# Causal attention with 16 heads: the mask added by VectorE on the way out of PSUM

## The reference, cut to what matters

```python
x = x + xattn(layernorm(x), ctx, ctx, ...)      # x, ctx: (16, 128, 256)
x = x + ffn(layernorm(x), w_fc, b_fc, w_proj, b_proj)

def xattn(q, k, v):                              # 16 heads of 16 features
    qh, kh, vh = q @ Wq.T + bq, k @ Wk.T + bk, v @ Wv.T + bv
    qh, kh, vh = (t.reshape(B, 16, 128, 16) for t in (qh, kh, vh))
    scores = einsum('bhqd,bhkd->bhqk', qh, kh) / sqrt(16)
    scores = where(triu(ones(128, 128), k=1), -inf, scores)
    out = einsum('bhqk,bhkd->bhqd', softmax(scores), vh)
    return out.reshape(B, 128, 256) @ Wp.T + bp

def ffn(x):                                      # 256 -> 1024 -> 256
    h = gelu(quant(x) @ quant(w_fc).T + b_fc)
    return quant(h) @ quant(w_proj).T + b_proj   # 3-bit mantissas, blocks of 32
```

## Time and profile before

| what | value |
|---|---|
| median of 3 runs | 295.81 us |
| the profiled execution | 296.32 us, span 294.3 us |
| PE busy | 248.6 us (84%) |
| PE weight loads | 176.6 us (60%) |
| DVE busy | 206.1 us (70%) |
| ACT busy | 168.0 us (57%) |
| POOL busy | 62.0 us (21%) |
| granted TensorE clock, mean | 0.915 |

### The profile page before, as it was taken

The page is one execution under the profiler, slowest core; times in us unless marked ns, Lnnn a source line. Parts: engine busy times, 40 slices in busy tenths (PEclk is TensorE's granted clock), DMA queues, the critical chain, the costliest instruction groups (busy, mean ns, idle before and its releaser), DMA issues.

```text
span 294.3 us, 6286 instructions
## 1 busy us (share of the span) xinstructions
PE 248.6 (84%) x2121; PEld 176.6 (60%) x2128; DVE 206.1 (70%) x435; ACT 168.0 (57%) x439; POOL 62.0 (21%) x54
## 2 busy tenths in 40 slices
PE   2764998998799899899999899788967974998853
PEld 1553776777577577578677677555733653565532
DVE  5400557979528857856956864896868999999991
ACT  2330665856726846855964864576843553676641
POOL 5200000000000100100100100335032354555551
PEclk9995799999779999999999799989775898699998
DMA  6457746755784565465555545443013001111111
GB/s 202 111 101 150 197 107 101 233 111 109 141 180 82 95 125 109 82 111 123 91 103 124 90 55 121 96 52 57 0 23 51 0 18 38 36 36 36 36 37 53
DMA packets 92436, 26.64 MB, mean 91 GB/s; under 512 B 69492, under 2 KB 92160, under 8 KB 92416
## 3 DMA queue, kind: packets, MB, share of 16 engines
q1 hardware_dynamic: 91328, 25.33, 42.3%
q10 hardware_dynamic: 1088, 1.05, 1.1%
HBM read 13.77 MB, written 8.39 MB: 75 GB/s over the span
## 4 chain that ended last, share of the span: by engine, by line
PE 51%; DVE 13%; ACT 11%; issue 9%; DMA 6%; SPq 5%; POOL 2%; POOLq 1%; ACTq 1%; DVEq 0%
PE bank L969 9%; PE bank L916 9%; ACT prob L411 7%; PE bank L980 7%; PE bank L963 4%; PE bank L1005 4%; PE bank L925 4%; PE bank L1123 3%; SPq L302 3%; PE bank L992 3%; DVE h_amax L841 2%; DMA scratch<-full 2%; PE bank L1121 2%; PE bank L1150 2%; DMA oden<-oT 2%
## 5 line engine op out<-in xcount | busy, mean ns | idle before, releaser
L411 ACT ACTIVATE prob<-bank,negm 128x128 f32<-128x128 f32 x256 | 69.6, 390 | 10.6 <-DVE negm L690 10.6
L690 DVE TENSOR_REDUCE negm<-bank 128x4 f32<-128x512 f32 x64 | 41.2, 685 | 42.6 <-PE bank L969 42.6
L417 ACT COPY probT<-bank 128x512 f32<-128x512 f32 x32 | 18.7, 583 | 52.0 <-PE bank L980 52.0
L969 PEld LDWEIGHTS bank<-k_mem,q_mem 16*128 16x128 f32 x512 | 33.7, 197 | 14.0 <-issue 14.0
L969 PE MATMUL bank<-k_mem,q_mem 16*128 16x128 f32 x512 | 40.1, 294 | 0.0
L980 PE MATMUL bank<-ident_f,prob 128*128 128x128 f32 x256 | 38.3, 297 | 0.0
L582 POOL TENSOR_TENSOR hq<-hrn,h_mag 128x1024 bf16<-128x1024 f32 x16 | 30.7, 1919 | 33.3 <-DVE hrn L852 33.3
L980 PEld LDWEIGHTS bank<-ident_f,prob 128*128 128x128 f32 x256 | 30.2, 150 | 4.0 <-issue 0.2
L963 PE MATMUL bank<-mask,ident_b 128*128 128x512 bf16 x64 | 19.8, 391 | 15.1 <-ACT prob L411 9.1
L505 ACT COPY hqT<-bank 128x1024 bf16<-128x1024 bf16 x16 | 16.2, 1012 | 20.3 <-PE bank L1138 20.3
L992 PE MATMUL bank<-probT,V 128*32 128x128 f32 x512 | 23.8, 290 | 3.9 <-DVE probT L695 3.2
(11 more groups left out here) (107 smaller groups left out, 397.2 us busy)
## 6 DMA issues: line engine op xcount, KB each, us to landing
scratch<-full SPq DMA_DIRECT2D x16, 256.0 KB, 3.1
oden<-oT SPq DMA_DIRECT2D x64, 64.0 KB, 2.5
k_mem<-scratch SPq DMA_DIRECT2D x32, 64.0 KB, 2.8
scratch_v<-vrow SPq DMA_DIRECT2D x16, 128.0 KB
q_mem<-scratch SPq DMA_DIRECT2D x32, 64.0 KB, 2.5
V<-scratch_v SPq DMA_DIRECT2D x16, 128.0 KB, 3.3
out<-res SPq DMA_DIRECT2D x16, 128.0 KB, 1.7
cbuf<-in_ctx SPq DMA_DIRECT2D x6, 256.0 KB, 3.2
```

The lines of the kernel that those rows point to most:

```text
L411: ins = nc.scalar.activation(prob[:, k % 4, g, :], score_b[k % 2][:, g * P:(g + 1) * P], ACT.Exp, bias=negm[:, k % 2, g:g + 1])
L690: V.tensor_reduce(negm[:, k % 2, :], score_b[k % 2][:, :].rearrange("p (g t) -> p g t", g=4), axis=AX.X, op=ALU.max, negate=True).then_inc ...
L969: ins = T.matmul(score_b[n][:, g * P:(g + 1) * P].rearrange("p (r j) -> p j r", r=RPH), QS[par][rows, cols], KS[par][rows, cols], start=Fa ...
```

## The change

The causal mask leaves PE and goes to DVE. The queries are scaled by -1/4 instead of 1/4, so the score banks hold negated scores, and the mask holds +1e30 above the diagonal. For each head DVE runs one fused instruction (`tensor_tensor_reduce`): it reads 128 x 128 negated scores out of PSUM, adds the mask, writes the sum to the head's slot of `prob` in SBUF, and keeps the row minimum, which is the negated row maximum of the scores. The exponentials then read and write `prob` in SBUF, with scale -1. `scores` of the next round waits for `masked` (the DVE instructions), no longer for `exp_done`. The wait for a free slot of `prob` moves from ACT to DVE. Both copies of the transposes are on ACT. `negm` has four slots instead of two.

```diff
@@ -47,7 +47,7 @@
         ident_b = sb("ident_b", [P, P], bf16)
         perm_f = sb("perm_f", [P, P])
         ones_b = sb("ones_b", [65, P], bf16)
-        mask = sb("mask", [P, P], bf16)
+        mask = sb("mask", [P, P])
         col_i = sb("col_i", [P, P], i32)
         col_f = sb("col_f", [P, P])
         colp_i = sb("colp_i", [P, P], i32)
@@ -61,6 +61,7 @@
         rowt_f = sb("rowt_f", [P, 1])
         neg_half = sb("neg_half", [P, 2])
         tick = sb("tick", [P, 1])
+        ticks = sb("ticks", [P, 4])
 
 
         w_rows = sb("w_rows", [P, 3, KC, E])
@@ -104,7 +105,7 @@
         QS = [sb(f"q_mem{n}", [P, NG // NR * P * HL]) for n in range(2)]
         KS = [sb(f"k_mem{n}", [P, NG // NR * P * HL]) for n in range(2)]
         V1 = [sb(f"V1_{n}", [P, 2, NH, 2 * HD]) for n in range(2)]
-        negm = sb("negm", [P, 2, 4])
+        negm = sb("negm", [P, 4, 4])
         prob = sb("prob", [P, 4, 4, P])
         probT = sb("probT", [P, 2, 4, P])
         oT = [sb(f"oT{n}", [P, NJ, 2, 4, RPH]) for n in range(2)]
@@ -144,7 +145,7 @@
             iota perm_set row_cast col_cast row_bits consts bias_scaled wT_in wT_out wp_permuted b_parts b_moved
             ones_set bn1 ag1 eps1 pow1 xn_ready tx_done tx_copied tc_done tc_copied
             proj_done proj_copied v_copied k_spilled q_spilled v_spilled q_stacked k_stacked v_stacked
-            s_done max_done exp_done t_done even_copied odd_copied av_done
+            s_done masked max_done exp_done t_done even_copied odd_copied av_done
             o_copied o_moved lden_done rden_done newton onrm_done y_done y_copied
             bn2 ag2 eps2 pow2 xn2_done amax2 exp2 mag2 round2 xq_done
             w_amax_done w_exp_done w_mag_done w_round fc_ready wtr_done wtr_copied
@@ -368,7 +369,7 @@
                     ins = nc.scalar.activation(grouped,
                                                proj_b[t][:, c * PT:(c + 1) * PT]
                                                .rearrange("p (r g h) -> p r g h", r=RPH, h=HL),
-                                               ACT.Identity, scale=(1.0, SCALE)[t],
+                                               ACT.Identity, scale=(1.0, -SCALE)[t],
                                                bias=bias_q[:, c:c + 1] if t else bias[:, 0, c:c + 1])
                 ins.then_inc(sm["proj_copied"], 1)
 
@@ -404,18 +405,21 @@
             copy_tc(1)
 
             def exps(i, k):
-                act.wait_ge(sm["max_done"], GROUPS * i + k + 1)
-                if k >= 4 or from_step(i, 1):
-                    act.wait_ge(sm["t_done"], GROUPS * i + k - 3)
+                act.wait_ge(sm["masked"], 4 * (GROUPS * i + k + 1))
                 for g in range(4):
-                    ins = nc.scalar.activation(prob[:, k % 4, g, :], score_b[k % 2][:, g * P:(g + 1) * P],
-                                               ACT.Exp, bias=negm[:, k % 2, g:g + 1])
+                    ins = nc.scalar.activation(prob[:, k % 4, g, :], prob[:, k % 4, g, :],
+                                               ACT.Exp, bias=negm[:, k % 4, g:g + 1], scale=-1.0)
                 ins.then_inc(sm["exp_done"], 1)
 
             def copy_even(i, j):
                 act.wait_ge(sm["t_done"], GROUPS * i + 2 * j + 1)
                 nc.scalar.copy(probT[:, 0, :, :].rearrange("p g t -> p (g t)"), probT_b[0][:, :])\
                     .then_inc(sm["even_copied"], 1)
+
+            def copy_odd(i, j):
+                act.wait_ge(sm["t_done"], GROUPS * i + 2 * j + 2)
+                nc.scalar.copy(probT[:, 1, :, :].rearrange("p g t -> p (g t)"), probT_b[1][:, :])\
+                    .then_inc(sm["odd_copied"], 1)
 
             def invert(p):
 
@@ -443,6 +447,7 @@
             def step(i, par):
                 if from_step(i, 1):
                     copy_even(i - 1, 3)
+                    copy_odd(i - 1, 3)
                 exps(i, 0)
                 exps(i, 1)
                 if from_step(i, 1):
@@ -450,6 +455,7 @@
                 if ahead(i):
                     copy_proj(i + 1, 0)
                 copy_even(i, 0)
+                copy_odd(i, 0)
                 exps(i, 2)
                 exps(i, 3)
                 if ahead(i):
@@ -457,6 +463,7 @@
                 if is_last(i):
                     copy_weights(0)
                 copy_even(i, 1)
+                copy_odd(i, 1)
                 exps(i, 4)
                 exps(i, 5)
                 copy_out(i, 0, par)
@@ -464,6 +471,7 @@
                     invert(i - 1)
                     copy_weights(1)
                 copy_even(i, 2)
+                copy_odd(i, 2)
                 exps(i, 6)
                 exps(i, 7)
                 if is_last(i):
@@ -477,6 +485,7 @@
 
             steps(act, step)
             copy_even(NPAIR - 1, 3)
+            copy_odd(NPAIR - 1, 3)
             copy_out(NPAIR - 1, 1, 1)
 
             def gelu(t, par):
@@ -648,10 +657,10 @@
             norm1(0)
             V.tensor_scalar(ident_b[:, :], col_f[:, :], row_f[:, :], None, ALU.is_equal).then_inc(sm["consts"], 1)
             dve.wait_ge(sm["row_cast"], 4)
-            V.tensor_scalar(mask[:, :], col_f[:, :], rowt_f[:, :], -BIG, ALU.is_gt, ALU.mult)\
+            V.tensor_scalar(mask[:, :], col_f[:, :], rowt_f[:, :], BIG, ALU.is_gt, ALU.mult)\
                 .then_inc(sm["consts"], 1)
             dve.wait_ge(sm["bias_in"], 64)
-            V.tensor_scalar(bias_q[:, :], bias[:, 1, :], SCALE, None, ALU.mult).then_inc(sm["bias_scaled"], 1)
+            V.tensor_scalar(bias_q[:, :], bias[:, 1, :], -SCALE, None, ALU.mult).then_inc(sm["bias_scaled"], 1)
             stats1(1)
             norm1(1)
             copy_v(0)
@@ -687,13 +696,13 @@
             def maxes(i, k):
 
                 dve.wait_ge(sm["s_done"], GROUPS * i + k + 1)
-                V.tensor_reduce(negm[:, k % 2, :], score_b[k % 2][:, :].rearrange("p (g t) -> p g t", g=4),
-                                axis=AX.X, op=ALU.max, negate=True).then_inc(sm["max_done"], 1)
-
-            def copy_odd(i, j):
-                dve.wait_ge(sm["t_done"], GROUPS * i + 2 * j + 2)
-                V.tensor_copy(probT[:, 1, :, :].rearrange("p g t -> p (g t)"), probT_b[1][:, :])\
-                    .then_inc(sm["odd_copied"], 1)
+                if k >= 4 or from_step(i, 1):
+                    dve.wait_ge(sm["t_done"], GROUPS * i + k - 3)
+                V.memset(ticks[:, k % 4:k % 4 + 1], 0.0)
+                for g in range(4):
+                    V.tensor_tensor_reduce(prob[:, k % 4, g, :], score_b[k % 2][:, g * P:(g + 1) * P], mask[:, :],
+                                           1.0, 3.0e38, ALU.add, ALU.min, negm[:, k % 4, g:g + 1])\
+                        .then_inc(sm["masked"], 1)
 
             def normalise(p):
 
@@ -778,8 +787,6 @@
                 one = type(i) is int and i == 1
                 maxes(i, 0)
                 maxes(i, 1)
-                if from_step(i, 1):
-                    copy_odd(i - 1, 3)
                 if from_step(i, 2):
                     normalise(i - 2)
                 if zero:
@@ -790,7 +797,6 @@
                     round_weights(0, 2)
                 maxes(i, 2)
                 maxes(i, 3)
-                copy_odd(i, 0)
                 if zero:
                     bias_parts(1)
                     copy_wp()
@@ -804,7 +810,6 @@
                     round_weights(1, 3)
                 maxes(i, 4)
                 maxes(i, 5)
-                copy_odd(i, 1)
                 if ahead(i):
                     copy_v(i + 1)
                 if zero:
@@ -818,7 +823,6 @@
                     round_weights(0, 3)
                 maxes(i, 6)
                 maxes(i, 7)
-                copy_odd(i, 2)
                 if zero:
                     round_weights(0, 0)
                 if one:
@@ -830,7 +834,6 @@
                     residual(i - 1)
 
             steps(dve, step)
-            copy_odd(NPAIR - 1, 3)
             quantise(NPAIR - 2)
 
 
@@ -958,16 +961,13 @@
             def scores(i, j, par):
 
                 if j or from_step(i, 1):
-                    pe.wait_ge(sm["exp_done"], GROUPS * i + 2 * j)
-                for n in range(2):
-                    T.matmul(score_b[n][:, :], ident_b[:, :], mask[:, :].unsqueeze(1).to_broadcast([P, 4, P]),
-                             start=True, stop=False)
+                    pe.wait_ge(sm["masked"], 4 * (GROUPS * i + 2 * j))
                 for g in range(4):
                     for n in range(2):
                         b, hs = heads(2 * j + n)
                         rows, cols = head_rows(b, hs[g])
                         ins = T.matmul(score_b[n][:, g * P:(g + 1) * P].rearrange("p (r j) -> p j r", r=RPH),
-                                       QS[par][rows, cols], KS[par][rows, cols], start=False, stop=(g == 3))
+                                       QS[par][rows, cols], KS[par][rows, cols], start=True, stop=True)
                         if g == 3:
                             ins.then_inc(sm["s_done"], 1)
 
```

## The result

The changed kernel took a median of 292.13 us (291.35 to 292.51, 4 runs) against 295.38 us before (294.16 to 300.44, 4 runs). The ratio is 0.990 with a 95% interval of 0.986 to 0.994, so it is about 1% faster, which lies within the 2% band of no change. In a later session the same pair gave 0.980 (0.975 to 0.985). The forecast was 293.5 us.

What follows compares the result with a forecast made beforehand. A ring of ACT and SP, 22.4 us against PE 19.1 and DVE 20.7, was to set the step. 1.9 + 2.4 - 1.8 = 2.5 us off 296.3 gives 293.8, forecast as a median of 293.5, range 290 to 299.

Steps and rivals of the forecast that it cites:

- ring around PE: ACT and SP, query spill to query spill through moves, logarithm and exponentials: sets the step, 22.4 us against 22.77 before.
- steps 0 and 1: Step 0 is PE work and gains up to 2.4 us without masks; step 1, nearly DVE's, loses 1.8.
- steps 2 to 6: Middle steps: each 0.37 us shorter, 5 x 0.37 = 1.9 us in all.
- The ring's sum: ACT and SP, query spill to query spill: terms add up to 22.4 us, with ends at 21.6 and 23.4.
- spill to landed moves: SP, query spill to landing of the eight attention output moves: 12.3 us taken, from 13.1 or 12.1 with quick moves.
- pair of 0.33: DVE, fused instruction plus 128 x 1 readout: 0.33 us, between 0.24 and 0.42; round 2.7, DVE's step 20.7.
- The rival of a bound DVE: DVE becomes the bound: pair of 0.44, round 3.58, step 24.2 us, kernel slower at 308; chance 0.20.
- The source in SBUF: ACT's exponentials reading SBUF: at most 0.05 us more each, 0.6 taken for the 16 in the ring around PE.
- PE's masks: PE loses mask matmuls of 0.60 us a round, 2.4 a step, so it needs 19.1 us instead of 21.5.
- PE's clock: Rival: more PE idle time brings low-clock stretches that catch the query projection, 10.4 us on top, 304; chance 0.12.
- the mark of 0.9: PE: a granted clock under 0.9 in 84 to 165 us would show that the falling-clock rival holds.
- my last warning: SP's queue: the forecast fails if the value gathers, last in it, come late for the attends, which now run earlier.

## Why the prediction was right, and where it was not

**That a ring around PE holds the changed kernel: right, and one run shows it. That it alone sets the step: not borne out.** The denominators' moves were put first, with every instruction of PE, ACT and DVE in place, and 7.5 us left the changed kernel's median, though in another session; in ratios to the kernel before, 0.950 against 0.980 and 0.990. That number had been forecast from the ring. The logarithm waited for the moves in six steps of the changed kernel, from 0.49 to 3.50 us. Against it stand three forecasts made from the same ring that failed. Taking two copies out of it gave nothing that shows, taking the logarithm off the moves gave nothing in the median, and putting the masks back on PE cost 7 us of the median where the ring allowed 1 to 2.5. PE's work and clock lie so close to the ring that what is taken from either shows only in part. That is what the prediction said of the two, and its sum then went by the longer one alone.

**The size: right, and partly by luck.** The profiled executions differ by 3.8 us of span, and the prediction had 2.5 by four terms. The query copies give them as follows:

| term | forecast | after |
|---|---|---|
| steps 0 and 1 | 2.4 - 1.8 = 0.6 | 0.17 |
| steps 2 to 6 | 1.9 | 1.40 - 0.17 = 1.23 |
| rest of the steps, step 7 above all | 0 | 2.52 - 1.40 = 1.12 |
| feed-forward layer | 0 | 3.8 - 2.52 = 1.3 |

Two terms came out smaller and two were not in the sum at all, and the last of these is no effect of the change.

**The ring's sum: 22.4 forecast, 22.86 in the chain, 22.96 on average.** Its terms on ACT were right. From the landing at 119.98 to the spill at 129.81 it took 9.83 us, where the terms had given 22.4 - 12.3 = 10.1:

| term | forecast | after |
|---|---|---|
| logarithm, inverse, both copies | 2.2 | 122.12 - 119.98 = 2.14 |
| exponentials of round 0, output copy | 2.8 | 124.94 - 122.12 = 2.82 |
| key copy | 0.9 | 0.73 |
| two copies | 1.0 | 126.60 - 125.67 = 0.93 |
| exponentials of round 1, query copy | 3.2 | 129.81 - 126.60 = 3.21 |

The mis-sized term is the first one, spill to landed moves. I took 12.3 from the quick moves of one step. It was 13.0 in this step, and 13.9 and 12.45 in the ones beside it, 13.1 on average, which was my high end. Steps 2 to 6 were to give 1.9 us. With the right term the ring is no shorter than before, and that is what steps 3 to 5 show; the 1.2 us of the five steps came in steps 2 and 6.

**DVE: pair of 0.33 forecast, 0.21 measured, under my low end of 0.24.** I added 0.05 for the readout to the whole row of the main one, on the ground that the readout needs the last element. The rows don't show that: readout and next main one start together, 0.07 before the row of the first main one ends. The plain instructions of 128 x 128 started 0.19 apart, so the readout costs 0.02 at most. DVE's step is then near 9.9 + 4 x 1.78 = 17.0 instead of 20.7. The term lay off the path, except that step 1 was to cost 1.8 by it. From the first `scores` of step 1 to those of step 2 it took 68.04 - 48.79 = 19.25, and 70.01 - 49.66 = 20.35 before, so that step cost nothing. The rival of a bound DVE fell with it. I had also written that the forecast fails if a pair lies outside 0.24 to 0.39: the pair did, and the forecast held, because DVE has time to spare. The Trainium skill, Vector Engine (DVE) Microarchitecture Reference, "Points that are easy to get wrong", states half the throughput for two SBUF sources that aren't bf16. With one of the two in PSUM no half rate shows here: 286 ns for 128 elements is the duration of the plain 128 x 128 instructions. The doubled pairs then priced the rival itself: at a round of 3.4 us the kernel took 313, not 308.

**The source in SBUF: right in size, wrong in where to look.** Eight exponentials took 2.45 us where they took 2.17, so 16 cost 0.56, and I had 0.6. But I said that a row would be 0.03 to 0.05 longer. The mean row is 396 ns against 390; it is the distance between two that grew.

**PE's masks: 2.4 us a step forecast, some 2.1 left.** A row of masks is 0.60 long, but the products start 0.53 behind its start (76.73 behind the 76.20 of the earlier trace rows), so its end lies under them. Four rounds are 2.1 us, and 17 us over the run where the rows give 19.2.

**Step 0: the 2.4 us did not come.** PE does set this step, as I had said. Its scores of round 1 had a lead of 0.85, mainly from masks that took 0.94 and 0.64 of the first two rounds, less a start that was 0.60 later. But the query copy of the step was 1.67 us late. PE's timeline, first before and then after:

```profile
34.51 1.09 PE L980 MATMUL bank<-ident_f,prob 128*128 128x128 f32 x8
35.44 1.89 PE L916 MATMUL bank<-xnT,wT 128*128 128x256 f32 x8
```
```profile
34.52 1.97 PE L980 MATMUL bank<-ident_f,prob 128*128 128x128 f32 x8
36.28 2.33 PE L919 MATMUL bank<-xnT,wT 128*128 128x256 f32 x8
```

PE was busy without a break in both. The granted clock from 34 to 38 us was 1.00 before and 0.61 after: the lower level at which both kernels begin their steps lasted longer in the changed one, and the scores of round 1, the transposes and the query projection together took 2.2 us more. The prediction priced these masks without the clock. Why the higher level came later is open.

**PE's clock: half of the rival came true.** The mean of the profiled execution fell from 0.915 to 0.905, and in the long stretch from 1.00 to 0.96, so the mark of 0.9 that I had set was not reached. But of the 17 to 19 us of PE work that left, 8 to 10 came back in longer matmuls. The timeline of PE, and then windows around it, show one of the stretches:

```profile
98.93 0.91 PE L992 MATMUL bank<-probT,V 128*32 128x128 f32 x16 [0.96 <-ACT probT L416]
...
102.47 3.35 PE L919 MATMUL bank<-xnT,wT 128*128 128x256 f32 x8
```
```profile
92.00:100.00 8.00, 6.25 (x70) 4.37 (x70) 6.89 (x42) 6.44 (x18) 1.31 (x2) 1.00 0.46 87
100.00:104.00 4.00, 3.82 (x28) 3.18 (x27) 3.31 (x25) 4.00 (x12) 0.00 (x0) 0.75 0.68 69
```

PE was busy for 6.25 of 8 us and had waited 0.96 us for a copy just before; then the query projection took 3.35 instead of 1.9. It may be that where the ring sets the step, PE's idle time grows with each us taken from it, and some of it returns as a lower clock. The rows fit that, and no run shows it. The Trainium skill, TensorE: Matmul & The Clock Gate, "A second HAM failure mode: psum-queue depth-cycling", says that short idle times between groups of matmuls, when they are frequent, make the clock swing between its levels, and this row agrees. The step from 106.95, where PE waited 0.42, 0.29, 0.26 and 0.18 us, has 1.00, so the rule alone doesn't tell when.

**What stays open.** Which wait triggers a low stretch; how the gain divides between the ring and PE's clock, since nothing held the clock fixed; and where the 1.1 us behind the query copy of step 6 come from. The gathers of the values, my last warning, came late only where the ring had been cut; whether moving them alone, with the denominators first, would give more was not tried.

## What to carry to other kernels

When two rings are almost equally long, price the change against the one that it does not shorten, and look for the cheapest edge in that one: here a new order of eight moves, with one semaphore split in two, was worth 3 to 4%, where taking 17 to 19 us of work from the busiest engine was worth 1 to 2%. Take the time from issue to landing as a mean over several steps, not from the quickest. Compare two kernels at a place that the change doesn't shift within a step, or part of the lead is only the shift. Before work is put "later", ask when its data arrives and what stands behind it on both engines that it connects.

## What the runs showed of the hardware

- A reduction kept beside a fused DVE instruction is read out by one of 128 x 1 that has a row of 83 ns and adds 0.02 us at most: pairs of 128 x 128 start 0.21 us apart, and plain instructions of that size started 0.19 apart.
- Exponentials of 128 x 128 follow each other 0.035 us slower out of SBUF than out of PSUM (2.45 against 2.17 us for eight), though their rows hardly differ.
- Less work on PE does not mean less PE time: mask rows of 19.2 us removed (17 us by their starts), 9.0 us of busy time gone. In the kernel with the denominators first the mean granted clock went along with the time (0.945 and 280.98 us, 0.897 and 292.16 us).
